# Spectral tower kernel on one core: the 32x32 tile sets wait for both pairs of PSUM banks together and go out as sixteen matmuls in one run

## The chip, the cores and the metric

The kernel runs on one core of a Trainium2 chip. The metric is the device time of one execution in microseconds (us). Three runs of the kernel before are given, beside one profiled execution. Engines: TensorE (PE, its weight loads PEld), VectorE (DVE), ScalarE (ACT), GpSimd (POOL), and SyncE (SP), which issues most transfers.

## What is computed

The reference puts 64 images of 64x64 through a small Fourier network (four layers, 32 channels), and the result through a short attention and mixture-of-experts stage on 65 tokens of 64 numbers. The part that matters here is the layer:

```python
for i in range(L):                       # L = 4
    x1 = _fourier_layer(v, W1, W2)       # rfft2, 24x12 modes mixed over channels, irfft2
    x2 = einsum('bcxy,cd->bdxy', v, w_w[i]) + w_b[i]
    v = x1 + x2
    v = batchnorm(v) * bn_g[i] + bn_b[i] # statistics over all images and positions
    if i < L - 1: v = relu(v)
```

After the layers come `q_w`, a class token, and a layernorm with the attention and the experts. Nothing of that tail is touched.

## The kernel before, in words

The maps don't fit on the chip, so each of the first three layers (`for l in range(PASSES)`, PASSES = 3) has two parts. `mix(l)` works on the modes. The pass that follows goes over the images in 16 groups of four ("quads", q = 0 to 15). It finishes layer l for the quad and begins layer l + 1: it builds the output map, clips it, stores it, transforms it forward to modes, and takes the channel product of the next layer only to gather its sum of squares, which that layer's normalisation needs.

A quad has two halves (h = 0 and 1). For each half the pass makes two sets of values in PSUM, both in banks 0 to 3:

- **Output set** (`out_set`): the channel product of layer l into banks 0 to 3, then 32 inverse-transform matmuls added to it (L1660). The channel product has three forms. In layer 0 it is four 32-row matmuls, one to a bank (L1646). In layers 1 and 2 it is `blocks32` (L1621) for q of 2 and more, and four full matmuls (L1637) for q = 0 and 1, which were kept on the chip.
- **Next set** (`next_set`): the channel product of layer l + 1 of the finished map, `blocks32` in every layer.

`blocks32` covers the 128x128 array with small matmuls of 32 rows and 32 columns; one of them (row group r, column group x) reads partitions 32r to 32r + 31 and writes bank r. Each is an fp32 matmul of 512 columns and stands in the trace as two records and two weight loads. In the kernel before it is called for a **pair** of banks: pair 0 is banks 0 and 1 (r = 0, 1), pair 1 is banks 2 and 3 (r = 2, 3), so eight matmuls per call, 16 records.

The pairs have semaphores of their own. `a_full[pair]` is raised when a pair is written, `a_free[pair]` when it has been read. `free_pair` (L1608) is the wait of TensorE for `a_free[pair]` of the set before. The readers of a set are:

| set | pair 0 | pair 1 |
|---|---|---|
| output, h = 0 | ACT relu (L1430) | DVE relu (L2036, then the clip L2039) |
| next, h = 0 | ACT square (L1439) | DVE bn_stats (L2045) |
| output, h = 1 | ACT relu (L1430) | ACT relu (L1430) |
| next, h = 1 | ACT square (L1439) | ACT square (L1439) |

So in the sets of h = 1 one engine reads pair 0 and then pair 1.

Banks 4 to 7 hold the forward transform: `y_transform` (L1683, 16 tiles of 32x32 at once, in two halves), and `x_transform` (L1695). Between them VectorE transposes (`turn_spectra`, L2074); it also transposes the finished map (`turn_map`, L2061) for `y_transform`.

TensorE runs its instructions in the order of the code. In this text the eight steps of one round are called A to H:

```python
for q in range(QUADS + 1):
    if q < QUADS: out_set(l, q, 0)          # A
    if q:
        y_transform(l, q - 1, 0)            # B
        next_set(l, q - 1, 0)               # C
        y_transform(l, q - 1, 1)            # D
    if q < QUADS: out_set(l, q, 1)          # E
    if q:
        x_transform(l, q - 1, 0)            # F
        next_set(l, q - 1, 1)               # G
        x_transform(l, q - 1, 1)            # H
```

ACT's order in a round is: relu of A (pair 0), square of C (pair 0), relu of E (both pairs), copy of F's result (L1447), square of G (both pairs), copy of H's result. DVE's order: relu and clip of A (pair 1), bn_stats of C (pair 1), two `turn_spectra`, two `turn_map`. SP stores each finished half map (L1160), loads the maps of later quads in layers 1 and 2 (L1166, awaited by `ld`), and loads the inverse spectra (L1171, awaited by `g_in`).

## Time and profile before

| | |
|---|---|
| three runs | 1352.03, 1356.14, 1361.01 us; median 1356.14 |
| the profiled execution | 1348.81 us, span of its instructions 1347.0 us |
| PE busy | 1134.5 us (84%), 18183 matmul records |
| PE weight loads | 646.0 us (48%) |
| DVE busy | 855.6 us (64%) |
| ACT busy | 551.6 us (41%) |
| POOL busy | 367.7 us (27%) |
| mean granted TensorE clock | 0.936 of full speed |

Busy time is the union of an engine's records. The idle time in square brackets of a row is that of the engine just before it, with what ended it. "issue" means that the profile shows nothing the engine waited for. Matmuls overlap in the array, so a group of x32 is one run of records.

### The profile page before, as it was taken

To read this page: it belongs to the slowest core of one execution; us is meant where nothing else is said; L and a number is where in the kernel's file an instruction comes from. 1 tells how busy PE (TensorE), PEld (TensorE's weight loads), DVE (VectorE), ACT (ScalarE), POOL (GpSimd) and SP (SyncE) were. 2 spreads that over 40 slices of the span, in tenths; PEclk is the share of its full clock that TensorE was granted. 3 is DMA by queue.
4 is the path that set the end of the run, shared out by engine and by line. 5 is a ranking of instruction groups with operands and counts; after the bars stand their busy time and mean duration, and the time that the engine had idled before them with its cause. 6 is when DMAs were issued, how large, how long until landed. Compare 5 with 4: busy or idle time off the path is not lost.

```text
span 1347.0 us, 40550 instructions
## 1 busy us (share of the span) xinstructions
PE 1134.5 (84%) x18183; PEld 646.0 (48%) x18183; DVE 855.6 (64%) x1041; ACT 551.6 (41%) x808; POOL 367.7 (27%) x533
## 2 busy tenths in 40 slices
PE   4698899999969889899996989999899677954596
PEld 4444555555534445555554445555455352223552
DVE  6576676777747566666764856666666480058664
ACT  2165454444536444444443644444444380100150
POOL 8673113224235303121422630122222351100000
PEclk9899899999989999999997999999999898976789
DMA  6568999898328999999962789999997267931001
GB/s 165 139 192 221 274 248 226 211 232 200 101 89 202 233 318 351 337 361 330 363 203 59 198 219 342 351 336 370 327 355 230 43 269 257 379 110 42 1 0 32
DMA packets 156119, 300.29 MB, mean 223 GB/s; under 512 B 33064, under 2 KB 100024, under 8 KB 139012
## 3 DMA queue, kind: packets, MB, share of 16 engines
q1 hardware_dynamic: 131656, 251.53, 60.8%
q0 software_dynamic: 20864, 44.73, 11.5%
q8 instruction: 143, 2.34, 0.7%
q10 hardware_dynamic: 3426, 1.44, 0.4%
q14 instruction: 30, 0.25, 0.1%
HBM read 147.86 MB, written 128.48 MB: 205 GB/s over the span
## 4 chain that ended last, share of the span: by engine, by line
PE 56%; DMA 12%; DVE 11%; SPq 8%; ACT 6%; issue 5%; POOL 2%; DVEq 0%; ACTq 0%; POOLq 0%
PE ps L1621 14%; PE ps L1660 10%; PE ps L1695 7%; PE ps L1683 6%; PE ps L1584 4%; SPq L1160 3%; PE ps L1646 3%; PE ps L1548 3%; DMA half_inverse<-arena 2%; DMA arena<-maps 2%; SPq L1054 1%; PE ps L1563 1%; DMA maps<-arena 1%; PE ps L1523 1%; ACT arena L1430 1%
## 5 line engine op out<-in xcount | busy, mean ns | idle before, releaser
L1660 PEld LDWEIGHTS ps<-arena 48*128 48x128 f32 x3072 | 182.2, 190 | 86.3 <-issue 82.2
L1660 PE MATMUL ps<-arena 48*128 48x128 f32 x3072 | 201.4, 281 | 7.3 <-issue 3.2
L1430 ACT ACTIVATE arena<-ps,arena 128x1024 f32<-128x1024 f32 x96 | 112.3, 1202 | 221.5 <-PE ps L1660 203.4
L1109 POOL DMA_DIRECT2D arena<-arena x207 | 120.4, 589 | 301.9 <-ACT arena L1447 298.0
L1439 ACT ACTIVATE ps<-ps 128x1024 f32<-128x1024 f32 x144 | 145.5, 1011 | 98.7 <-PE ps L1621 98.4
L2074 DVE STREAM_TRANSPOSE arena<-ps 128x1024 f32<-128x1024 f32 x96 | 177.3, 1929 | 5.5 <-PE ps L1683 5.5
L1621 PE MATMUL ps<-arena 32*32 32x512 f32 x2944 | 160.3, 616 | 9.3 <-DMA arena<-maps 5.6
L1683 PE MATMUL ps<-arena 32*32 32x512 f32 x3072 | 152.2, 599 | 5.6 <-DVE arena L2061 3.4
L2061 DVE STREAM_TRANSPOSE arena<-arena 128x2048 f32<-128x2048 f32 x64 | 144.3, 2289 | 12.8 <-issue 6.4
L1695 PE MATMUL ps<-arena 128*64 128x96 f32 x2304 | 122.8, 257 | 32.7 <-DVE arena L2074 29.8
L1695 PEld LDWEIGHTS ps<-arena 128*64 128x64 f32 x2304 | 103.7, 142 | 87.6 <-issue 47.2
L1255 POOL TENSOR_SCALAR arena<-arena 32x384 f32<-32x384 f32 x96 | 112.4, 1171 | 83.4 <-DMA arena<-in_mode_w 77.1
L2036 DVE TENSOR_SCALAR arena<-ps,arena 128x1024 f32<-128x1024 f32 x32 | 43.0, 1343 | 117.5 <-PE ps L1660 117.5
L1621 PE MATMUL ps<-inputs,arena 32*32 32x512 f32 x1920 | 107.9, 613 | 7.7 <-issue 6.7
L1548 PE MATMUL ps<-arena 64*64 64x64 f32 x2304 | 79.9, 287 | 33.2 <-DMA arena<-arena 31.0
L1430 ACT ACTIVATE inputs<-ps,arena 128x1024 f32<-128x1024 f32 x48 | 56.1, 1202 | 120.7 <-PE ps L1660 120.7
L1548 PEld LDWEIGHTS ps<-arena 64*64 64x64 f32 x2304 | 65.3, 155 | 82.8 <-issue 71.6
L1249 POOL DMA_DIRECT2D arena<-in_mode_w x48 | 26.8, 566 | 260.0 <-ACT arena L1447 242.8
L2045 DVE BATCH_NORM_STATS2 arena<-ps 128x6 f32<-128x512 f32 x96 | 62.3, 690 | 40.9 <-PE ps L1621 40.9
L2061 DVE STREAM_TRANSPOSE arena<-inputs 128x2048 f32<-128x2048 f32 x32 | 72.5, 2308 | 8.1 <-ACT inputs L1430 4.0
L1621 PEld LDWEIGHTS ps<-arena 32*32 32x32 f32 x2944 | 39.7, 104 | 79.1 <-ACT arena L1430 30.0
L1035 ACT COPY arena<-ps 128x1024 f32<-128x1024 f32 x66 | 56.2, 857 | 50.2 <-PE ps L1584 50.2
(314 smaller groups left out, 1394.4 us busy)
## 6 DMA issues: line engine op xcount, KB each, us to landing
arena<-half_inverse SPq DMA_DIRECT2D x90, 384.0 KB, 12.1
half_inverse<-arena SPq DMA_DIRECT2D x120, 256.0 KB, 4.6
maps<-arena SPq DMA_DIRECT2D x112, 256.0 KB, 4.6
maps<-inputs SPq DMA_DIRECT2D x112, 256.0 KB, 12.4
arena<-maps SPq DMA_DIRECT2D x28, 1024.0 KB, 17.3
maps<-arena SPq DMA_DIRECT2D x28, 1024.0 KB, 18.0
inputs<-maps SPq DMA_DIRECT2D x28, 1024.0 KB, 21.7
arena<-in_mode_w POOLq DMA_DIRECT2D x48, 384.0 KB, 7.2
```

The costliest lines, as they stand in the source:

```text
L1109: eng.dma_start(dst, src).then_inc((modes_st[batch % 2], last_st, late_st)[part], 16)
L1255: nc.gpsimd.tensor_scalar(w, w, -1.0, None, ALU.mult).then_inc(signed, 1)
L1430: nc.scalar.activation(half(h_out(l, q), h)[:, 1024 * pair:1024 * pair + 1024], ps[:, 2 * pair:2 * pair + 2, :].rearrange("p b n -> p (b n ...
L1439: nc.scalar.activation(src, src, ACT.Square, accum_out=sums_x2[:, i:i + 1])\
L1548: last = nc.tensor.matmul(ps[64 * e:64 * e + 64, 2 * s + m, 0:384] .rearrange("p (b k) -> p k b", b=BATCH)[:, k], ring[2 * p + e][rows, 6 ...
L1621: last = nc.tensor.matmul(ps[32 * x:32 * x + 32, r, :], w[rows, 32 * r:32 * r + 32], source[rows, at:at + 512], start=True, stop=last_one)
L1660: last = nc.tensor.matmul(ps[:, b, at:at + 128], gtile[s][rows, 4 * b + 2 * h + n, :], iy[rows, :], start=False, stop=(i >= 2 and n == 1))
L1683: last = nc.tensor.matmul(ps[32 * x:32 * x + 32, 4 + r, :], fyt[rows, yh, :], src, start=(yh == 0), stop=(yh == 1))
L1695: last = nc.tensor.matmul(ps[64 * t:64 * t + 64, 4 + b, 96 * (y - 3 * b):96 * (y - 3 * b) + 96], spectra[:, at:at + 64], fx2[:, r, :], sta ...
L2045: last = nc.vector.bn_stats(stats[:, 12 * q + 6 * b:12 * q + 6 * b + 6], ps[:, 2 + b, :])
L2061: nc.vector.transpose(dst, src).then_inc(h_turned, 1)
L2074: nc.vector.transpose(dst, src).then_inc(y_turned, 1)
```

## The change

`blocks32` no longer takes a pair. It goes over the four column groups and, within each, over all four row groups: sixteen matmuls in a run. Before it TensorE waits for both pairs. `a_full[0]` is raised by the matmul of x = 3, r = 1, and `a_full[1]` by that of x = 3, r = 3. In layer 0 the four matmuls of the output set also follow both waits. The branch of layers 1 and 2 for the two kept quads (L1637) is left as it was.

```diff
-            def blocks32(w, source, h, pair, last_one):
+            def blocks32(w, source, h, done):
+
                 for x in range(4):
-                    for r in (2 * pair, 2 * pair + 1):
+                    for r in range(4):
                         rows = slice(32 * r, 32 * r + 32)
                         at = 2048 * h + 512 * x
-                        last = nc.tensor.matmul(ps[32 * x:32 * x + 32, r, :], w[rows, 32 * r:32 * r + 32],
-                                                source[rows, at:at + 512], start=True, stop=last_one)
-                return last
+                        ins = nc.tensor.matmul(ps[32 * x:32 * x + 32, r, :], w[rows, 32 * r:32 * r + 32],
+                                               source[rows, at:at + 512], start=True, stop=done)
+                        if done and x == 3 and r % 2:
+                            ins.then_inc(a_full[r // 2], 1)
...
                     for pair in range(2):
                         free_pair(l, "out", q, h, pair)
-                        blocks32(wbd[l], h_in(l, q), h, pair, False)
+                    blocks32(wbd[l], h_in(l, q), h, False)
...
                     for pair in range(2):
                         free_pair(l, "out", q, h, pair)
-                        for g in (2 * pair, 2 * pair + 1):
-                            rows = slice(32 * g, 32 * g + 32)
-                            nc.tensor.matmul(ps[:, g, :], expconv[rows, at:at + 128],
-                                             feats[u][rows, 512 * h:512 * h + 512], start=True, stop=False)
+                    for g in range(4):
+                        rows = slice(32 * g, 32 * g + 32)
+                        nc.tensor.matmul(ps[:, g, :], expconv[rows, at:at + 128],
+                                         feats[u][rows, 512 * h:512 * h + 512], start=True, stop=False)
...
                 for pair in range(2):
                     free_pair(l, "next", q, h, pair)
-                    blocks32(wbd[l + 1], h_out(l, q), h, pair, True).then_inc(a_full[pair], 1)
+                blocks32(wbd[l + 1], h_out(l, q), h, True)
```

Lines behind L1616 move: what is L1621, L1660, L1683 and L1695 before is L1622, L1662, L1685 and L1697 after.

What TensorE's row of instructions is at steps F, G, H and the next A, in layer 1, before the change:

```order
L1695 MATMUL ps<-arena 64x96 [waits y_turned]
L1695 MATMUL ps<-arena 64x96 x11
L1621 MATMUL ps<-inputs,arena 32x512 [waits a_free0]
L1621 MATMUL ps<-inputs,arena 32x512 x7
L1621 MATMUL ps<-inputs,arena 32x512 [waits a_free1]
L1621 MATMUL ps<-inputs,arena 32x512 x7
L1695 MATMUL ps<-arena 64x96 [waits y_turned]
L1695 MATMUL ps<-arena 64x96 x11
L1621 MATMUL ps<-arena 32x512 [waits a_free0,ld_a0]
L1621 MATMUL ps<-arena 32x512 x7
L1621 MATMUL ps<-arena 32x512 [waits a_free1]
L1621 MATMUL ps<-arena 32x512 x7
```

The same place after it:

```order
L1697 MATMUL ps<-arena 64x96 [waits y_turned]
L1697 MATMUL ps<-arena 64x96 x11
L1622 MATMUL ps<-inputs,arena 32x512 [waits a_free1,a_free0]
L1622 MATMUL ps<-inputs,arena 32x512 x15
L1697 MATMUL ps<-arena 64x96 [waits y_turned]
L1697 MATMUL ps<-arena 64x96 x11
L1622 MATMUL ps<-arena 32x512 [waits a_free1,a_free0,ld_a0]
L1622 MATMUL ps<-arena 32x512 x15
```

The eight matmuls of pair 0 now stand behind the wait for pair 1, and the first matmul of the run carries one wait more.

TensorE at steps B, C and D, in layer 1, before the change:

```order
L1683 MATMUL ps<-arena 32x512 [waits y_turned,xs_ev,h_turned]
L1683 MATMUL ps<-arena 32x512 x15
L1621 MATMUL ps<-inputs,arena 32x512 [waits a_free0]
L1621 MATMUL ps<-inputs,arena 32x512 x7
L1621 MATMUL ps<-inputs,arena 32x512 [waits a_free1]
L1621 MATMUL ps<-inputs,arena 32x512 x7
L1683 MATMUL ps<-arena 32x512 [waits y_turned,xs_ev,h_turned]
L1683 MATMUL ps<-arena 32x512 x15
```

After it:

```order
L1685 MATMUL ps<-arena 32x512 [waits y_turned,xs_ev,h_turned]
L1685 MATMUL ps<-arena 32x512 x15
L1622 MATMUL ps<-inputs,arena 32x512 [waits a_free1,a_free0]
L1622 MATMUL ps<-inputs,arena 32x512 x15
L1685 MATMUL ps<-arena 32x512 [waits y_turned,xs_ev,h_turned]
L1685 MATMUL ps<-arena 32x512 x15
```

The order of the steps is unchanged; nothing moves past B or D, and ACT, DVE, POOL and SP have the same instructions in the same order.

## Rows read from the trace of the kernel before

**Rows 1.** Busy time by stretch, steady part of passes 0 and 1; columns named in row.

```profile
core 0: us, PE busy (x) PEld busy (x) DVE busy (x) ACT busy (x) POOL busy (x), PEclk, DMA share, GB/s
144.00:372.00 228.00, 219.23 (x3800) 130.96 (x3800) 167.90 (x120) 108.18 (x163) 54.82 (x82) 1.00 0.82 209
480.00:715.00 235.00, 215.66 (x4296) 122.17 (x4280) 160.38 (x113) 104.92 (x157) 54.74 (x82) 0.99 0.95 317
```

**Rows 2.** Timeline, pass 0: start us, us, engine line op, operands, count [idle before <-releaser].

```profile
190.00 1.34 DVE L2036 TENSOR_SCALAR arena<-ps,arena 128x1024 f32<-128x1024 f32 x1 [3.51 <-PE ps L1660]
190.82 0.29 PEld L1621 LDWEIGHTS ps<-arena 32*32 32x32 f32 x16 [0.78 <-ACT arena L1430]
191.40 0.18 PEld L1621 LDWEIGHTS ps<-arena 32*32 32x32 f32 x16 [0.28 <-DVE arena L2036]
191.99 1.62 PE L1683 MATMUL ps<-arena 32*32 32x512 f32 x30
192.59 1.30 DVE L2045 BATCH_NORM_STATS2 arena<-ps 128x6 f32<-128x512 f32 x2 [0.52 <-PE ps L1621]
...
196.74 2.30 ACT L1430 ACTIVATE arena<-ps,arena 128x1024 f32<-128x1024 f32 x2 [3.57 <-DMA maps<-arena]
...
198.68 0.18 PEld L1621 LDWEIGHTS ps<-arena 32*32 32x32 f32 x16
199.09 0.18 PEld L1621 LDWEIGHTS ps<-arena 32*32 32x32 f32 x16 [0.23 <-ACT arena L1430]
199.88 1.01 ACT L1439 ACTIVATE ps<-ps 128x1024 f32<-128x1024 f32 x1 [0.55 <-PE ps L1621]
...
200.89 1.02 ACT L1439 ACTIVATE ps<-ps 128x1024 f32<-128x1024 f32 x1
202.07 0.30 PEld L1646 LDWEIGHTS ps<-inputs,arena 32*128 32x128 f32 x4 [0.51 <-ACT ps L1439]
```

**Rows 3.** Timeline, pass 0, step G one round earlier, pair 1.

```profile
183.79 0.18 PEld L1621 LDWEIGHTS ps<-arena 32*32 32x32 f32 x16 [0.23 <-ACT arena L1430]
```

**Rows 4.** Timeline, passes 1 and 2, step G in five rounds.

```profile
479.67 0.18 PEld L1621 LDWEIGHTS ps<-inputs,arena 32*32 32x32 f32 x16 [0.70 <-ACT inputs L1430]
...
529.72 0.18 PEld L1621 LDWEIGHTS ps<-inputs,arena 32*32 32x32 f32 x16 [0.79 <-ACT inputs L1430]
529.95 1.01 ACT L1439 ACTIVATE ps<-ps 128x1024 f32<-128x1024 f32 x1
...
1021.35 0.18 PEld L1621 LDWEIGHTS ps<-arena 32*32 32x32 f32 x16 [0.79 <-ACT arena L1430]
...
1053.46 0.51 PEld L1621 LDWEIGHTS ps<-arena 32*32 32x32 f32 x32
```

**Rows 5.** Timeline, pass 1, ACT frees pair 0 and step E begins.

```profile
706.21 0.19 ACT L1439 ACTIVATION_READ_ACCUMULATOR ps<-ps 128x1 f32 x1
...
706.52 0.24 PEld L1621 LDWEIGHTS ps<-arena 32*32 32x32 f32 x16 [0.59 <-issue]
```

**Rows 6.** Timeline, pass 1, a step G with both pairs free.

```profile
596.88 0.23 PEld L1621 LDWEIGHTS ps<-inputs,arena 32*32 32x32 f32 x32
...
598.08 1.01 ACT L1439 ACTIVATE ps<-ps 128x1024 f32<-128x1024 f32 x1 [0.69 <-PE ps L1621]
```

**Rows 7.** Waits of the weight loads by line, passes 0, 1, 2: total us, times, longest.

```profile
PEld ps L1621 <- issue: 1.9, 2, 1.6
...
PEld ps L1621 <- issue: 15.9, 20, 2.9
...
PEld ps L1621 <- issue: 19.3, 28, 2.1
```

**Rows 8.** Timeline, end of pass 1: steps B and C, both pairs free.

```profile
715.65 0.27 PEld L1683 LDWEIGHTS ps<-arena 32*32 32x32 f32 x32 [1.32 <-DVE arena L2061]
...
716.54 0.57 PEld L1621 LDWEIGHTS ps<-inputs,arena 32*32 32x32 f32 x31 [0.33 <-issue]
...
717.92 1.01 ACT L1439 ACTIVATE ps<-ps 128x1024 f32<-128x1024 f32 x1 [2.34 <-PE ps L1621]
```

## The prediction

> **What bounds the kernel now.** I read the busy time by stretch first. In the steady part of pass 0 PE is busy 219.23 of 228.00 us and DVE 167.90; in pass 1 it is 215.66 of 235.00 and 160.38 [rows 1]. That looks like PE as the bound, but overlapping matmuls are counted as busy while they drain, so I read the timeline of one round for who waits for whom [rows 2]. The reader should follow this loop:
>
> - C: ACT frees pair 0, and PE starts it at 190.82. DVE's relu runs from 190.00 to 191.34, and PE starts pair 1 at 191.40.
> - DVE's bn_stats follow, 192.59 to 193.89, and free pair 1 for E.
> - E's relu runs on ACT from 196.74 to 199.04 (two of 1.2 us), pair 0 first. The row names a store of the maps as releaser. I set that aside: in the code the relu of A in the same round has already waited for the same value of that semaphore, so at E only E's matmuls are left to wait for.
> - G: PE starts pair 0 at 198.68, straight behind F, and pair 1 at 199.09, released by that relu.
> - ACT's squares of G start at 199.88 and 200.89, back to back, and PE starts pair 1 of the next A at 202.07, released by the second square.
>
> A round is 15.30 us long (pair 1 of G at 183.79 and at 199.09) [rows 2, 3]. In each of C, E and A, pair 1 is the late one and lies on the loop; an early pair 0 gains nothing there. G is the exception. Its pair 0 starts 0.41 us before pair 1, ACT reads both pairs in turn, and what ends last is pair 0's start plus two squares. So the early pair 0 of G is worth its whole lead.
>
> **The change part by part.** Matmuls, weight loads and bytes are the same. What changes is when pair 0 starts, how long a run is, and how many waits the first matmul has.
>
> *G waits for both pairs.* The square begins 1.20 us after the start of pair 0 (198.68 to 199.88) [rows 2]. A run of both pairs that were free together shows the same 1.20 us (596.88 to 598.08) [rows 6]. With both waits ahead the run begins at 199.09, the first square at 200.29 instead of 199.88, and everything behind it is 0.41 us later: second square, A, relu, C, bn_stats, E. Nothing hides it, since the two squares already stand back to back and A already waits for the second.
>
> In passes 1 and 2 the lead of pair 0 varies. It is the idle time in the row of pair 1 plus the 0.18 us of pair 0's own loads. I count the 30 full rounds in three classes [rows 4]. In 11 rounds the lead is 0.85 to 0.97 us, on average 0.94 (first: 0.70 + 0.18 = 0.88 at 479.67; last: 0.79 + 0.18 = 0.97 at 1021.35). These are rounds whose E came late, so that ACT was still in its relus when F was done. There the loss is also the whole lead: the square at 529.95 would start at 529.72 + 1.20 = 530.92. In 9 rounds the lead is about 0.33 (the run of 0.51 us at 1053.46, less 0.18). In the other ten it is small: eight of about 0.11, one of 0.62, and one whose cause is an instruction stall that remains, counted as nothing. Sum: 11 x 0.94 + 9 x 0.33 + 8 x 0.11 + 0.62 = 14.8 us.
>
> *A run of sixteen instead of eight from the late release.* The sixteen weight loads of a pair take 0.18 us, the 32 of both pairs 0.23 [rows 2, 6], so the last matmul starts 0.05 us later. Bounds: nothing, if the reader waits for pair 0 only, and 0.05. I take 0.05, for C and G in pass 0 and for all four sets in passes 1 and 2. The four-matmul form of layer 0 adds next to nothing.
>
> The Trainium skill's page "TensorE: Matmul & The Clock Gate", section on the measured speedup against the span model, puts each further packed tile at about 4 ns. By it eight more tiles cost 0.03 us instead of 0.05, about 3 us less in the uncovered sum; the row's 6 ns decides.
>
> *One wait more on the first matmul.* A set whose single wait ends releases PE 0.06 us later (191.34 to 191.40) [rows 2]. Where the first matmul has two waits, as at E in pass 1, the square ends at 706.40 and the loads begin at 706.52, so 0.12 [rows 5]. In the new order every set begins with two waits or more, the late one among them. I charge the difference, 0.06 us, four times a round. Bounds: 0, if the late wait is still taken last and directly, and 0.12.
>
> *Sum.* A round of pass 0 gets 0.41 + 2 x 0.05 + 4 x 0.06 = 0.75 us longer. Thirteen of its 15 rounds are of that kind, and two had another hold-up at G and pay 0.34: 10.4 us. Passes 1 and 2 pay 14.8 + 30 x 4 x 0.11 = 28.0 us if nothing covers it.
>
> *What may cover it.* In pass 1 the DMA queues are at a share of 0.95 (0.82 in pass 0) [rows 1], and the loads of L1621 wait 15.9 us in 20 places, and 19.3 us in 28 in pass 2, for nothing the profile names, against 1.9 us in 2 in pass 0 [rows 7]. I take these for instructions that arrive late behind the data. A PE that comes later at such a place waits less there, so a delay ahead of it is partly paid already. No row says how large a part; with 20 and 28 such waits in some 14 rounds each, there are one or two a round to pay into, but not behind every delay. I let half of the 28.0 go: 14.0 us. Bounds: none and all of it.
>
> Together 10.4 + 14.0 = 24.4 us on the profiled execution's 1348.8 (span 1347.0 and 1.8 around it), so 1373. The median of the runs, 1356.1, stands 7.3 above that execution; the same step gives 1380, which is 1.8% slower. A measurement of this kernel can tell about 1%, 13.6 us, from no change.
>
> **The rivals.**
>
> *Nothing is covered, or the stalls grow.* PE used to pass pair 0 early and so called for its next instructions early; now it stands in front of the set and then takes sixteen matmuls in a burst. For it: stalls of up to 2.9 us inside such sets [rows 7]. Against it: PE also has longer to be supplied. Price: 38.4 us, 1394.
>
> *The busy passes cover all.* If late data and late instructions pace passes 1 and 2, their rounds stay as long as they are, and only pass 0 pays: 10.4 us, 1366, under 1%. For it: DMA share 0.95. Against it: many rounds there have the same closed loop of G, squares and A, with no wait for DMA in it.
>
> *Not slower: PE's array time decides.* Where both pairs are free when PE arrives, two half runs are worse than one, because pair 1 queues behind pair 0 while a y_transform is still in the array. At the end of pass 1 B starts at 715.65 and the square of C at 717.92, 2.27 us [rows 8]; at most 1.0 us for the B run and the 1.20 above would give 2.20 or less, so 0.1 to 0.3 us saved at C and the like at E behind D. That decides from the point where PE, not ACT or DVE, is last at C and E. With 0.3 us in each of 30 rounds and the loss at G gone (both pairs free there too) it is -9 us, 1347. Against it: in the round of rows 2 PE waits 0.78 us for pair 0 of C and 0.28 for pair 1, and D is done at 193.61, before bn_stats at 193.89. The skill's same section speaks for this rival: sixteen packed tiles of 32x32 cost hardly more than one. The trace agrees (1.20 us for eight and for sixteen), but the array isn't what the loop waits for.
>
> That the change doesn't do what it says is excluded by the new order of the instructions.
>
> **How the numbers follow.** Forecast, half covered (a quarter to three quarters: 1373 to 1388): 0.50. Nothing covered, 1394: 0.17. All covered, 1366: 0.20. Not slower, 1347: 0.08. The remaining 0.05 is for what I don't see, on both sides. Slower by over 1% takes the first two and a part of the rest, 0.68; within 1% the next two, 0.28; faster by over 1% 0.04. The range of 1362 to 1395 leaves out the last rival, and the tail of the worst. The likeliest is 1380.
>
> **What would show it.** In the profile after, G has one run of 32 loads behind ACT's second relu, and the first square starts about 1.25 us behind that; the round of pass 0 is 16.05 instead of 15.30 (15.8 would mean that the additional wait costs nothing); PE waits about 0.4 to 0.5 us more a round for ACT's square (A), and DVE as much more for A's L1662. The waits of L1622 on nothing named should shrink in passes 1 and 2; if they don't, the first rival is right. I am wrong if the round of pass 0 stays at 15.30, if the squares of G aren't back to back any longer, or if the granted clock of the steady stretches falls from 1.00 and 0.99 (2.4 GHz), since PE now stands idle longer before each A.

## The result, and the profile after

The changed kernel takes 1403.34 us (median of 4 runs, 1400.87 to 1411.13) where the kernel before takes 1357.01 (4 runs, 1352.03 to 1361.01): a ratio of 1.0347, 95% interval 1.030 to 1.0393. It is 3.5% slower. The forecast had 1380 and a range of 1362 to 1395: the sign was right, the time lies outside the range, and the forecast had half of the loss that came. The ratios here and below leave out the few executions that took over 1.5% longer than the fastest of the same kernel.

The profiled execution of the changed kernel takes 1401.0 us (span 1399.2, mean granted clock 0.927), so it stands 52.2 above that of the kernel before. In what follows "a round" is one q, and the steps are A to H as ahead of the prediction. A pass is measured from the last matmul of its first set to the release of its last one. Read so, the three passes take 273.4, 287.7 and 294.6 us, against 256.2, 274.0 and 272.8: 17.2, 13.7 and 21.8 us more. That is the whole difference; between the passes and behind them nothing moved by more than half a microsecond. (How far the single passes can be trusted is a question for before_again below.)

The busy time by stretch, kernel after, answers [rows 1]:

```profile
core 0: us, PE busy (x) PEld busy (x) DVE busy (x) ACT busy (x) POOL busy (x), PEclk, DMA share, GB/s
144.00:372.00 228.00, 184.16 (x3552) 109.11 (x3550) 157.46 (x112) 101.71 (x152) 45.87 (x66) 0.99 0.84 206
480.00:715.00 235.00, 188.59 (x3938) 107.41 (x3938) 149.81 (x105) 96.61 (x144) 46.87 (x67) 0.98 1.01 322
```

PE falls from 219 to 184 busy microseconds in pass 0, although a round has the same matmuls. Most of that isn't lost time: before, pair 0's run filled the stretch in which pair 1 was waited for, and now PE stands idle there and the same matmuls stand closer together. What is lost shows on DVE, 168 to 157 in pass 0 and 160 to 150 in pass 1, which does the same work per round: rounds are 6 to 7% longer. The granted clock of each stretch is 0.01 lower than before.

Two groups of section 5 of the pages (line, operation, operands, count, busy and mean, idle ahead and its releaser). The kernel before:

```profile
L1439 ACT ACTIVATE ps<-ps 128x1024 f32<-128x1024 f32 x144 | 145.5, 1011 | 98.7 <-PE ps L1621 98.4
L2045 DVE BATCH_NORM_STATS2 arena<-ps 128x6 f32<-128x512 f32 x96 | 62.3, 690 | 40.9 <-PE ps L1621 40.9
```

and the kernel after:

```profile
L1439 ACT ACTIVATE ps<-ps 128x1024 f32<-128x1024 f32 x144 | 145.5, 1011 | 158.9 <-PE ps L1622 158.9
L2047 DVE BATCH_NORM_STATS2 arena<-ps 128x6 f32<-128x512 f32 x96 | 62.3, 690 | 46.6 <-PE ps L1622 46.6
```

The readers of the next layer's products wait longer for them: ACT 158.9 us in all instead of 98.7, DVE 46.6 instead of 40.9.

The timeline of one round of pass 0, kernel after, with the columns of [rows 2], from one C over the next G to the bn_stats of the next C:

```profile
196.00 0.27 PEld L1622 LDWEIGHTS ps<-arena 32*32 32x32 f32 x32 [1.42 <-ACT arena L1430]
...
201.63 2.30 ACT L1430 ACTIVATE arena<-ps,arena 128x1024 f32<-128x1024 f32 x2 [3.20 <-PE ps L1662]
...
204.04 0.27 PEld L1622 LDWEIGHTS ps<-arena 32*32 32x32 f32 x32 [0.71 <-issue]
204.07 1.15 PE L1622 MATMUL ps<-arena 32*32 32x512 f32 x32 [0.55 <-ACT arena L1430]
205.36 1.01 ACT L1439 ACTIVATE ps<-ps 128x1024 f32<-128x1024 f32 x1 [1.14 <-PE ps L1622]
206.37 1.02 ACT L1439 ACTIVATE ps<-ps 128x1024 f32<-128x1024 f32 x1
207.61 0.34 PEld L1648 LDWEIGHTS ps<-inputs,arena 32*128 32x128 f32 x8 [1.44 <-issue]
207.64 1.14 PE L1648 MATMUL ps<-inputs,arena 32*128 32x512 f32 x8 [1.28 <-ACT ps L1439]
210.89 1.34 DVE L2038 TENSOR_SCALAR arena<-ps,arena 128x1024 f32<-128x1024 f32 x1 [4.33 <-PE ps L1662]
212.35 0.27 PEld L1622 LDWEIGHTS ps<-arena 32*32 32x32 f32 x32 [1.42 <-ACT arena L1430]
212.38 1.15 PE L1622 MATMUL ps<-arena 32*32 32x512 f32 x32 [0.54 <-DVE arena L2038]
213.66 1.01 ACT L1439 ACTIVATE ps<-ps 128x1024 f32<-128x1024 f32 x1 [2.00 <-PE ps L1622]
213.72 1.30 DVE L2047 BATCH_NORM_STATS2 arena<-ps 128x6 f32<-128x512 f32 x2 [0.76 <-PE ps L1622]
```

C begins at 196.00 and again at 212.35: the undisturbed round is 16.35 us, where the prediction said 16.05 and the kernel before has 15.30 [rows 2, 3]. Going along it against [rows 2]:

- **C.** DVE's relu ends at 210.89 + 1.34 = 212.23, and the first load starts at 212.35, 0.12 behind it (0.06 before). The matmul starts another 0.03 behind its load. The bn_stats start 1.37 behind the load (192.59 - 191.40 = 1.19 before). Together 0.24 us more from relu to bn_stats.
- **G.** The relu of both pairs ends at 201.63 + 2.30 = 203.93; load at 204.04, square at 205.36. From relu to square that is 1.43, against 199.88 - 199.04 = 0.84: 0.59 more, of which 0.41 is the lead that pair 0 had.
- **A.** The second square ends at 207.39 and the load starts at 207.61, 0.22, against 202.07 - 201.91 = 0.16; with the 0.03 to the matmul some 0.1 more.
- **E.** By the same working from the trace 0.11 more.

0.24 + 0.59 + 0.10 + 0.11 = 1.04 of the 1.05 us. The form "one run of 32 loads behind ACT's second relu, then squares back to back" is as forecast; the joint set is dearer than forecast at every place.

The waits of the weight loads, kernel after, answer [rows 7]: those of L1622 on nothing named, in the steady parts of passes 0, 1 and 2 (us in total, times, longest), then those of L1648 (A and E) in pass 0:

```profile
PEld ps L1622 <- issue: 11.8, 16, 1.3
...
PEld ps L1622 <- issue: 47.2, 44, 1.5
...
PEld ps L1622 <- issue: 48.1, 44, 3.4
...
PEld ps L1648 <- issue: 39.6, 29, 1.4
```

The prediction said that these waits would shrink. In passes 1 and 2 they grew to 2.5 to 3 times what they were [rows 7], but the row doesn't mean what I had taken it for. At 204.04 the load waited 0.71 us "for issue" while the matmul behind it waited for ACT: it is the wait for the relu, under another name. Run late_first below shows why.

### The profile page after: what moved, and what is told of

The parts are those of the page before. It is cut to its first block, busy times and chain, and to the rows that moved or that the text cites. A ratio compares the mean times of both kernels' runs of the same rounds, so it can differ in the third digit from the quotient of the medians.

```text
span 1399.2 us, 40678 instructions
## 1 busy us (share of the span) xinstructions
PE 1081.0 (77%) x18183; PEld 620.0 (44%) x18183; DVE 855.0 (61%) x1041; ACT 552.1 (39%) x808; POOL 367.2 (26%) x533
## 3 DMA queue, kind: packets, MB, share of 16 engines
q8 instruction: 144, 2.36, 0.7%
## 4 chain that ended last, share of the span: by engine, by line
PE 49%; DVE 16%; ACT 16%; issue 8%; DMA 6%; SPq 3%; POOL 1%; DVEq 0%; ACTq 0%; POOLq 0%
PE ps L1622 13%; PE ps L1662 12%; ACT ps L1439 7%; ACT arena L1430 4%; PE ps L1584 4%; PE ps L1548 3%; DVE arena L2038 3%; DMA maps<-arena 3%; PE ps L1648 2%; ACT inputs L1430 2%; PE ps L1639 2%; DVE arena L2047 2%; PE ps L1697 2%; PE ps L1563 2%; SPq L1086 2%
## 5 line engine op out<-in xcount | busy, mean ns | idle before, releaser
L1662 PEld LDWEIGHTS ps<-arena 48*128 48x128 f32 x3072 | 187.2, 193 | 95.1 <-issue 93.6
L1662 PE MATMUL ps<-arena 48*128 48x128 f32 x3072 | 207.9, 285 | 12.7 <-issue 10.4
L1439 ACT ACTIVATE ps<-ps 128x1024 f32<-128x1024 f32 x144 | 145.5, 1011 | 158.9 <-PE ps L1622 158.9
L1622 PE MATMUL ps<-arena 32*32 32x512 f32 x2944 | 116.8, 620 | 51.0 <-ACT ps L1439 16.5
L1697 PE MATMUL ps<-arena 128*64 128x96 f32 x2304 | 126.4, 262 | 31.0 <-DVE arena L2076 26.5
L1697 PEld LDWEIGHTS ps<-arena 128*64 128x64 f32 x2304 | 106.5, 145 | 86.4 <-issue 49.9
L1685 PE MATMUL ps<-arena 32*32 32x512 f32 x3072 | 135.0, 608 | 8.6 <-issue 8.5
L2038 DVE TENSOR_SCALAR arena<-ps,arena 128x1024 f32<-128x1024 f32 x32 | 43.0, 1343 | 139.4 <-PE ps L1662 139.4
L1622 PE MATMUL ps<-inputs,arena 32*32 32x512 f32 x1920 | 76.9, 609 | 41.0 <-ACT ps L1439 17.8
L1249 POOL DMA_DIRECT2D arena<-in_mode_w x48 | 26.8, 564 | 284.5 <-ACT arena L1447 267.5
L2047 DVE BATCH_NORM_STATS2 arena<-ps 128x6 f32<-128x512 f32 x96 | 62.3, 690 | 46.6 <-PE ps L1622 46.6
L1622 PEld LDWEIGHTS ps<-arena 32*32 32x32 f32 x2944 | 28.4, 104 | 103.0 <-issue 64.7
```

The lines of the kernel that those rows point to most:

```text
L1439: nc.scalar.activation(src, src, ACT.Square, accum_out=sums_x2[:, i:i + 1])\
L1622: ins = nc.tensor.matmul(ps[32 * x:32 * x + 32, r, :], w[rows, 32 * r:32 * r + 32], source[rows, at:at + 512], start=True, stop=done)
L1662: last = nc.tensor.matmul(ps[:, b, at:at + 128], gtile[s][rows, 4 * b + 2 * h + n, :], iy[rows, :], start=False, stop=(i >= 2 and n == 1))
L1685: last = nc.tensor.matmul(ps[32 * x:32 * x + 32, 4 + r, :], fyt[rows, yh, :], src, start=(yh == 0), stop=(yh == 1))
L1697: last = nc.tensor.matmul(ps[64 * t:64 * t + 64, 4 + b, 96 * (y - 3 * b):96 * (y - 3 * b) + 96], spectra[:, at:at + 64], fx2[:, r, :], sta ...
L2047: last = nc.vector.bn_stats(stats[:, 12 * q + 6 * b:12 * q + 6 * b + 6], ps[:, 2 + b, :])
```

## The experiments

Each group of kernels ran on one chip with the kernel before beside them, so each ratio is to the kernel before of the same group. There are ten runs. The diffs show the heart of each edit; `...` stands for like edits elsewhere and for helper functions that only spell out a loop over a pair or over both.

In every run whose steady round was forecast, the round came within 0.15 us of it. The times didn't fit as well: they were off by up to 19 us, on either side. What is said of the round of pass 0 is therefore better founded than what is said of the whole time.

### The part of step G: g_split and g_only

g_split is the changed kernel with G's pairs apart again; g_only is the kernel before with G alone joined.

```diff
 def next_set(l, q, h):
+    if h == 1:
+        for pair in range(2):
+            free_pair(l, "next", q, h, pair)
+            pair32(wbd[l + 1], h_out(l, q), h, pair)
+        return
...
```

> The kernel after, with the next set of h = 1 (step G) alone back in two pairs with their own waits. Theory: of the 1.05 us by which a round of pass 0 grew (15.30 to 16.35), 0.59 lie at G: the lead of pair 0 of 0.41 and 0.18 of costs of a joint set. So the round should be 15.76 us, and the kernel about 28 us shorter than after, some 1373 to 1375. Rival: a run of sixteen matmuls is itself slow, the same in each of the four sets of a round, and the lead of pair 0 counts for little; then taking one of four away gives back a quarter, a round of 16.09 and about 1390 us.

Measured: 1389.56 us (1377.36 to 1408.34, 5 runs), ratio 1.0236 (1.0134 to 1.0338). The steady round of pass 0 is 15.65, so G gives back 0.70 of the 1.05 us, and the three passes take 262.5, 284.0 and 288.9. The round speaks for the theory (15.76 against 16.09); the median is that of the rival (1390), and 15 us above the theory's. Passes 1 and 2 gave back 3.7 and 5.7 us in the profiles, less than G's leads there; how much of that is chance can't be told from one profile (see before_again).

```diff
 def next_set(l, q, h):
+    if h == 1:
+        for pair in range(2):
+            free_pair(l, "next", q, h, pair)
+        joint32(wbd[l + 1], h_out(l, q), h)
+        return
...
```

> The kernel before, with step G alone made joint: both waits, then sixteen matmuls. Theory: a round of pass 0 of 15.30 + 0.59 = 15.89 us, and about 28 us more than before in the whole, some 1385. Rival (every joint set costs alike): 15.56 us and about 1369.

Measured: 1374.66 us (4 runs), ratio 1.0145 (1.0073 to 1.0216), round 15.90. G joined in the kernel before costs 0.60 us a round, as the theory had it; the time is 10 us under the theory's. The timeline of g_only, one G of pass 0:

```profile
198.42 2.30 ACT L1430 ACTIVATE arena<-ps,arena 128x1024 f32<-128x1024 f32 x2 [3.56 <-DMA maps<-arena]
...
200.83 0.28 PEld L1630 LDWEIGHTS ps<-arena 32*32 32x32 f32 x32 [0.61 <-issue]
202.15 1.01 ACT L1439 ACTIVATE ps<-ps 128x1024 f32<-128x1024 f32 x1 [1.14 <-PE ps L1630]
```

Relu to square is 202.15 - 200.72 = 1.43, as in the kernel after, and C, E and A are as in the kernel before. So the effects are separable: the losses of g_only and g_split are 1.45% and 2.36%, together 3.8% against 3.5% for the whole. What follows: the lost lead at G is real, but with its 0.41 us it is less than half of the 1.05. The rest is a dearer joint set, at G itself and at the three sets where, by the prediction, pair 0's early start was worth nothing.

### The order of the two waits: late_first

A set that waits for both pairs names pair 0 and then pair 1 in the code, and pair 1 is the late one. Here the late one is named first, in output sets and next sets alike. In the output sets both waits also move ahead of those for the inputs (`conv_exp` and `f_in` in layer 0, `ld` in layers 1 and 2), which stood first.

```diff
 def next_set(l, q, h):
-    for pair in range(2):
+    for pair in (1, 0):
         free_pair(l, "next", q, h, pair)
     blocks32(wbd[l + 1], h_out(l, q), h, True)
...
```

> The kernel after, with nothing changed but the order of the waits in the code before each joint set: pair 1 (the late one) first, pair 0 and the loads behind it, so that the wait that ends last is carried by the first weight load and not by an instruction of its own ahead of it. Theory: that instruction costs 0.07 us a set, so a round of pass 0 of 16.35 - 4 x 0.07 = 16.07 and about 12 us less in the whole, 1391. Rival: two waits cost the same in either order, 16.35 and 1403.

Measured: 1382.22 us (1377.97 to 1384.87, 4 runs), ratio 1.019 (1.0122 to 1.0258), against 1.0347: about 1.5% of the time back for the order of the waits. The round is 16.00 (16.07 was expected), the time 9 us under the theory's. The timeline of late_first, one C of pass 0:

```profile
192.23 1.34 DVE L2038 TENSOR_SCALAR arena<-ps,arena 128x1024 f32<-128x1024 f32 x1 [4.06 <-PE ps L1662]
...
193.63 0.24 PEld L1622 LDWEIGHTS ps<-arena 32*32 32x32 f32 x32 [1.36 <-DVE arena L2038]
193.63 1.15 PE L1622 MATMUL ps<-arena 32*32 32x512 f32 x32 [0.45 <-DVE arena L2038]
...
194.98 1.30 DVE L2047 BATCH_NORM_STATS2 arena<-ps 128x6 f32<-128x512 f32 x2 [0.68 <-PE ps L1622]
```

The relu ends at 193.57 and the load starts 0.06 behind, as in [rows 2]; its matmul starts with it, not 0.03 later. That is 0.09 us a set, and four sets make the 0.35 us of the round. Where the late wait had been shows in the instructions at L1610, the line of that wait, over the same 244 us of pass 0. Kernel after:

```profile
L1610 PEldq EVENT_SEMAPHORE  x88: 51/51/51, 146.3 to 385.9; - x88
```

and late_first:

```profile
L1610 PEldq EVENT_SEMAPHORE  x30: 51/51/51, 152.4 to 385.1; - x30
```

Which semaphore each record waits for is in the trace as well, though the views above leave it out. In the kernel after, the weight load of C and G carries the wait for pair 0, and a separate instruction ahead of it, 51 ns long, waits for pair 1. At A and E the load carries the wait for `conv_exp`, the first in the code, pair 0 has a separate instruction, and pair 1 shares one with the input. So the first wait of the code is carried by the weight load itself, and the others sit on instructions of their own ahead of it. Of the 88 rows, 30 at C and G and 29 at A and E name pair 1: but for one, these are four sets in 15 rounds, and every joint set has its late wait in the slow place. In late_first none has. Its 30 rows at L1610 name pair 0, which is free earlier, at C and G, and the separate instructions of A and E stand at the lines of the waits for the inputs. The kernel before has 29 rows here, all at A and E, and none names pair 1.

This also explains the rows above. In late_first the waits of L1648 have their names back:

```profile
PEld ps L1648 <- ACT ps L1439: 19.4, 14, 1.4
PEld ps L1648 <- DVE arena L2047: 18.6, 15, 1.2
```

19.4 + 18.6 = 38.0 us in 29 waits, where the kernel after shows 39.6 "for issue" in 29. A wait that ends on the separate instruction isn't the load's own, and the profile finds no releaser for it, or a wrong one: at C the row of 212.35 names ACT, which freed pair 0 about 0.6 us before, where DVE's relu is what ended the wait. In late_first the same wait stands under DVE L2038, 20.2 us in 15 places.

### The same wait without joint sets: two_waits

The kernel before, with one more wait ahead of pair 1's, for pair 0, which is long satisfied. It puts the late wait of each pair 1 in the second place; the matmuls stay as they are.

```diff
 def free_pair(l, kind, q, h, pair):
     if SETS[kind, q, h]:
+        if pair:
+            pe.wait_ge(a_free[0], set_of(l, kind, q, h))
         pe.wait_ge(a_free[pair], set_of(l, kind, q, h))
```

> The kernel before, with a second wait, one that is long satisfied (that of pair 0), ahead of the wait of pair 1, in every set; the first weight load of pair 1 carries the satisfied one. Matmuls stay in pairs. Theory: pair 1 is late on the loop in C, E and A, each by 0.07 us, and not at G: a round of pass 0 of 15.30 + 0.21 = 15.51 and 9 us more than before, 1366. Rival: a wait more costs nothing, 15.30 and 1357; then the costs of a joint set are all in its sixteen matmuls.

Measured: 1384.72 us (1378.87 to 1399.15, 4 runs), ratio 1.0227 (1.0137 to 1.0317), round 15.47. The timeline of two_waits, a C of pass 0:

```profile
193.32 1.34 DVE L2038 TENSOR_SCALAR arena<-ps,arena 128x1024 f32<-128x1024 f32 x1 [4.41 <-PE ps L1662]
...
194.78 0.21 PEld L1623 LDWEIGHTS ps<-arena 32*32 32x32 f32 x16 [0.34 <-issue]
...
196.00 1.30 DVE L2047 BATCH_NORM_STATS2 arena<-ps 128x6 f32<-128x512 f32 x2 [0.60 <-PE ps L1623]
```

Relu to load is again 0.12 and load to bn_stats 1.22 instead of 1.19, with pairs apart. So the 0.09 belongs to the wait's place and not to the run of sixteen. Of four such sets a round only 0.17 us reaches the round, not 0.35. The working for that is at split_late. But the time rose by 2.3%, far more than 45 rounds of 0.17, and 19 us more than expected: the passes take 264.0, 286.5 and 299.4 in the profiled execution, which was the slowest of the four. In pass 2 the loads wait longer for nothing named. Two_waits:

```profile
PEld ps L1623 <- issue: 34.2, 56, 3.7
PEld ps L1662 <- issue: 27.2, 30, 1.7
```

Much of the first row is the misnamed wait again, in 56 places. I also added up the intervals of over 0.6 us from the start of one TensorE record to the start of the next, where the next has no wait at all; these can't be misnamed. Below they are called stalls, though a part of each is the array at work. In the three passes they come to 6.3, 16.5 and 32.9 us, against 2.6, 12.0 and 16.9 in the kernel before. Why the third pass of this kernel has twice the stalls isn't explained.

### Which part of the time is pass 0: pass0_only

The change applied in pass 0 alone.

```diff
 def next_set(l, q, h):
+    if l:
+        for pair in range(2):
+            free_pair(l, "next", q, h, pair)
+            pair32(wbd[l + 1], h_out(l, q), h, pair, True)
+        return
...
```

> The change in pass 0 alone; passes 1 and 2 in pairs as before. The changed kernel's profile has pass 0 longer by 17.2 us, pass 1 by 13.7 and pass 2 by 21.8. Theory: each pass pays by itself, in every round, and nothing covers it: pass 0 at 273.4 us against 256.2, passes 1 and 2 at about 273 each as before, in the whole 17 us more than before, some 1369 to 1371. Rival: part of what passes 1 and 2 lost comes down to them from pass 0 (the clock, the stores of pass 0 still under way), then they grow here too and the time is nearer 1385.

Measured: 1375.91 us (1370.4 to 1382.64, 4 runs), ratio 1.014 (1.0041 to 1.024). Pass 0 is 273.5 us and its round 16.35, as in the kernel after. The clean loop of pass 0, which the forecast put at 10.4 us, costs 17.3. The passes that keep the old order take 284.0 and 279.0 in this execution, 10 and 6 us more than in the first profile of the same instructions, so the profile alone doesn't exclude the rival. The median is 5 us above the theory's and 9 under the rival's, and the interval has room for both. That asked for a control.

### How far the busy passes vary by themselves: before_again

> The kernel before, unchanged, as a control. The steady round of pass 0 should be 15.30 us again and pass 0 256 us within 1. What is open is how far the stalls of PE inside its runs in passes 1 and 2 (12.0 and 16.9 us in the first profile) vary for the same instructions. If they are a property of the program, they come out within 3 us of these numbers, and the larger stalls of the experiments are caused by their edits. If they vary from one execution to the next, they come out off by 5 us or more in one of the passes, and differences of that size between the profiles of two kernels say nothing. The time is 1357 within its usual 0.7% either way.

Measured: 1362.42 us (1349.5 to 1368.19, 10 runs), ratio 1.0023 (0.9986 to 1.006), as it must. Its passes take 254.7, 278.4 and 276.2 us, its steady round is 15.30. Its stretch of pass 1, against [rows 1]:

```profile
core 0: us, PE busy (x) PEld busy (x) DVE busy (x) ACT busy (x) POOL busy (x), PEclk, DMA share, GB/s
480.00:715.00 235.00, 214.17 (x4207) 121.05 (x4194) 155.02 (x111) 100.78 (x152) 54.08 (x81) 0.97 0.99 315
```

The same instructions get 155.02 us of DVE work done there instead of 160.38. The stalls on PE come to 0.7, 18.0 and 18.7 us, where the first profile had 2.6, 12.0 and 16.9. The second case of the expectation holds: in one execution the stalls of a busy pass are worth no more than plus or minus 6 us. With pass0_only there are three profiles of the old order in passes 1 and 2: 274.0, 278.4 and 284.0 us, and 272.8, 276.2 and 279.0. So a busy pass of one profile is known to 10 us, and the first profile, from which the prediction was made, has the shortest of both. Pass 0 varies by 1.5 us in all and its steady round by 0.01, so everything below 10 us in this study is read from the round of pass 0 or from medians.

With that scale, the stalls of the kernel after, 3.4, 15.6 and 18.2 us, can't be told from those of the kernel before. They didn't shrink by the 14 us that the forecast had let them take up, and they didn't grow.

### Who is late behind a joint set: r_swapped, pair_major and roles

From load to bn_stats, C has 1.19 before and 1.35 even in late_first. The sixteen-load run explains 0.05 of that. The suspicion: both pairs are now signalled within a few nanoseconds (13 by the ends of the matmuls in the trace, which are modelled), and the second signal is passed on late. The rival was that ACT and DVE, which now start on the two pairs of PSUM at the same time, are in each other's way. r_swapped takes the row groups in the order 2, 3, 0, 1, so that pair 1 is signalled first.

```diff
-                    for r in range(4):
+                    for r in (2, 3, 0, 1):
```

> The kernel after, with the row groups of the joint run in the order 2, 3, 0, 1 instead of 0, 1, 2, 3, so that the signal of pair 1 is raised 13 ns before that of pair 0 and not behind it. At step C in the changed kernel VectorE begins its bn_stats 0.19 us behind the last matmul of pair 1, where it was 0.10 before. Theory: two signals raised within 13 ns are passed on one after the other, and the second is late; then VectorE is back at 0.10 here, C's part falls by 0.09 us, and ScalarE's square of C and of G starts up to 0.09 later, so the round stays about 16.35. Rival: both readers start on PSUM at once and the second to start is held up by the first; then VectorE's delay stays what it is, or goes to whoever starts second. Time within 5 us of after in both.

The timeline of r_swapped, a C of pass 0:

```profile
195.74 0.28 PEld L1622 LDWEIGHTS ps<-arena 32*32 32x32 f32 x32 [1.42 <-ACT arena L1430]
...
197.06 1.30 DVE L2047 BATCH_NORM_STATS2 arena<-ps 128x6 f32<-128x512 f32 x2 [0.70 <-PE ps L1622]
197.12 1.01 ACT L1439 ACTIVATE ps<-ps 128x1024 f32<-128x1024 f32 x1 [2.07 <-PE ps L1622]
```

In the kernel after ACT starts 1.31 behind the load and DVE 1.37; here DVE starts 1.32 behind it and ACT 1.38. Over the rounds of pass 0 (medians at C), ACT starts 145 ns behind the end of its pair and DVE 192 in the kernel after; swapped, it is 190 and 146. (In the kernel before 37 and 104.) The delay goes with the order of the signals. At C that doesn't decide, since the reader that is signalled second also starts second, and the expectation gave this outcome to the rival as well. G decides: ACT alone reads both pairs there. Its first square starts 107 ns behind the end of pair 0 in the kernel before and 146 in the kernel after, where pair 0 is signalled first; swapped, where it is signalled last, it is 191, with no other reader of these banks to be in its way. So the rival falls. DVE's return to 104, which the theory had, didn't come. The time didn't change: 1403.77 us (2 runs), ratio 1.036 (1.0231 to 1.0488), round 16.35.

pair_major keeps both waits ahead but issues pair 0's eight and then pair 1's eight, so the signals are 62 ns apart.

```diff
-                for x in range(4):
-                    for r in range(4):
+                for x, r in [(x, 2 * pair + i) for pair in range(2) for x in range(4) for i in range(2)]:
```

> The kernel after, with both waits ahead of the run as there, but the eight matmuls of pair 0 first and then the eight of pair 1. The two signals then are some 50 ns apart instead of 13, and pair 0 is full 40 ns earlier. Theory (what a joint run costs is its start and its length): pair 0 of G is full 0.04 us earlier and VectorE's delay at C shrinks from 0.19 to about 0.12, a round of pass 0 of about 16.25. Rival (the order over row groups matters for how fast the array takes sixteen): the round moves by more than 0.15 either way.

A miss. ACT's delay falls to 93 ns, but DVE's stays at 192, where about 0.12 us was expected; 1403.81 us (2 runs), ratio 1.036 (1.0224 to 1.0496). The round of the profile is 16.40, but it can't be held against the 16.25 expected: this execution had a lower granted clock throughout, never over 0.95 where all the other profiles reach 1.00. Its steady part of pass 0:

```profile
144.00:388.00 244.00, 200.76 (x3792) 117.59 (x3792) 167.70 (x120) 108.02 (x161) 54.88 (x82) 0.94 0.80 196
```

The packed matmuls take 618 ns there instead of 588, and A and E, which the edit doesn't touch in pass 0, are 0.04 us longer each. Without these the round would be 16.32 or less (an estimate from these rows); whether the edit gains at full clock is open.

What is shown: behind a joint set DVE, signalled last, starts some 90 ns later than in the kernel before (192 against 104), ACT as the one signalled last just as late (190, against 37 at C and 107 at G), and 62 ns between the signals don't help. Why is open; being closer than 62 ns isn't the condition.

roles is the kernel before with the readers exchanged where h is 0: DVE takes pair 0 and ACT pair 1, so that the longer pair of operations starts first. It was the one idea in the study for a kernel better than both.

```diff
-                for pair in range(2 if h else 1):
+                for pair in (0, 1) if h else (1,):
...
```

> The kernel before, matmuls in pairs, with the readers of the sets of h = 0 exchanged: VectorE (relu 1.34 us, clip, bn_stats 1.30) takes pair 0, which an output set fills 0.45 us before pair 1, and ScalarE (relu 1.20, square 1.01 + 0.19) takes pair 1. No arithmetic is left out. Theory (the loop goes through whichever pair of C is free last): VectorE frees pair 0 at about the time at which ScalarE freed it before, plus 0.15, ScalarE frees pair 1 about 0.15 earlier than VectorE did, bn_stats start up to 0.45 earlier, and E waits for ScalarE's square, ready about 0.25 us earlier than bn_stats were. A round of pass 0 of 15.05 us and 10 us less than before, 1344. Rival: the loop is closed by another limb (turn_spectra, F, G), and the round stays at 15.30.

The round of pass 0 falls to 15.04, as expected, and pass 0 to 251.1 us. The time is 1352.74 us (median of 10 runs, one of which was far off at 2432.93), ratio 0.9968 (0.9921 to 1.0016): no difference that can be told, where 10 us were expected. In this profile pass 1 took 284.5 us, and its stalls came to 25.4.

### Both costs taken back: split_late

g_split and late_first in one kernel: G in pairs, and the three joint sets C, E and A with the late wait first (and, as in late_first, ahead of those for the inputs).

> The kernel after with both costs taken back that the earlier runs separated: G waits pair by pair again (g_split), and the three joint sets C, E and A take their late wait first in the code (late_first). If the two costs are independent, the steady round of pass 0 is g_split's 15.65 less three times the 0.09 us that late_first gained per joint set, 15.38, and the time is g_split's 1389.6 less three quarters of late_first's gain of 21.1 us, 1374. Rival: the gain of late_first comes from G alone (from the lead that G loses); then the round stays at 15.65 and the time within 5 us of 1389.

Measured: 1369.47 us (1360.18 to 1385.67, 12 runs), ratio 1.0076 (1.0041 to 1.0111); passes 261.3, 275.0 and 284.4. The rival falls, by the time and by the round (15.65 in g_split): the order of the waits gains with G in pairs as well. The time is within 5 us of what was expected. The round is 15.48 and not 15.38, and the trace tells why. The timeline of split_late, a G of pass 0:

```profile
199.46 2.30 ACT L1430 ACTIVATE arena<-ps,arena 128x1024 f32<-128x1024 f32 x2 [3.11 <-DMA maps<-arena]
...
201.39 0.18 PEld L1632 LDWEIGHTS ps<-arena 32*32 32x32 f32 x16
...
201.81 0.18 PEld L1632 LDWEIGHTS ps<-arena 32*32 32x32 f32 x16 [0.24 <-ACT arena L1430]
202.59 1.01 ACT L1439 ACTIVATE ps<-ps 128x1024 f32<-128x1024 f32 x1 [0.54 <-PE ps L1632]
```

The first loads of G (201.39) follow F without idle time; their wait, for the first of the two relus, ended long before. What times them is F ahead of them on PE, not the relu, so the square at 202.59 hangs on F. A relu of E that comes 0.11 later is caught there: from that relu to the release of G is 2.87 us in g_split and in two_waits, 2.96 in split_late, 2.98 in the kernel before. In a kernel with G in pairs, a delay at E is free, up to the lead. So removing it gains nothing. What three sets gain, 3 x 0.09, less the 0.09 that G loses, is the 0.17 us by which the round is shorter than g_split's 15.65; in two_waits the same sum appears with the other sign. With G joined there is no such cover, and all four sets pay. That part of G's price was in no step of the prediction.

What is left of split_late over the kernel before, 15.48 - 15.30 = 0.18 us, stands at C (0.05 for the run of sixteen, about 0.1 for the later second reader). Forty-five rounds of it are 8 us, and by the ratio the time is 10 above.

## Why the prediction was right or wrong

**The loop and the place.** Right. The chain of G, its two squares, A, C's relu, bn_stats and E sets the round before and after. Pair 0's lead at G is worth its whole length: g_only gives 0.60 a round for G, of which 0.41 is left when the terms below (0.09, 0.05, 0.04) are taken off. Early pairs 0 in E and A gain nothing by themselves: in late_first, where the late wait is carried directly, E and A are each only 0.01 us longer than in the kernel before.

**A run of sixteen, 0.05.** Right in size. The loads of both pairs take 0.24 us in late_first, where the wait is carried directly, and those of one pair 0.18 before. At C and at G it reaches the reader.

**One wait more, 0.06 four times a round.** Too small. It is 0.09: 0.06 until the load, as read from [rows 5], and 0.03 more until the matmul, which no row of the prediction held. late_first measures it directly, 0.35 us in four sets. The bounds given for this step were 0 and 0.12, and they hold; 0 was for the case that "the late wait is still taken last and directly". It is taken last and not directly.

**The second reader.** Missing from the sum. About 0.09 us at C, and 0.04 at G: two signals at the end of one run, where there had been one behind each. The Trainium skill's page "TensorE: Matmul & The Clock Gate", section on the per-tile semaphore tail, says that increments at the end of a packed group serialize, at about 26 ns each. One increment more in the group of C would by that figure cost 1.2 us in 45 rounds, an estimate from the page. The trace doesn't agree in size: the reader signalled last is 88 ns later than before, and stays so with the signals 62 ns apart.

Together the joint sets cost 0.64 us a round beside the lead, where the sum had 0.34.

**Half of it covered in passes 1 and 2.** This is the step that failed worst. It read, "I let half of the 28.0 go: 14.0 us", because the loads of L1621 wait there for instructions [rows 7]. With the sizes measured in pass 0 the two passes should lose 14.8 for the leads and 30 x 0.64 = 19.2, so 34.0 us uncovered (an estimate; the sizes weren't read in these passes). The first two profiles show 13.7 + 21.8 = 35.5, but that agreement is partly luck, since a busy pass of one profile is known to 10 us. The medians are the better witness: 46.3 us for the whole, less 17.3 for pass 0, leave 29.0 for passes 1 and 2, and with the interval of the ratio 23 to 36. So they lost twice the 14.0, and of the 34.0 nothing to a third was covered, not half. The stalls inside PE's runs show no difference beyond their own 6 us either. The mistake is in the reasoning, too: a stall that appears in a place where PE has nothing else to wait for doesn't get shorter because PE arrives later, unless its instructions were on their way meanwhile, and no row said that they were. (That is argument: no run shows what the stalls wait for.) I had written "No row says how large a part" and then took the middle; the rows for a part of nothing were as good.

**The sum.** On the profiled executions the forecast had +24.4 and the change brought +52.2. Of the 27.8 between them, 14.0 is the cover, 6.8 is pass 0 (17.2 instead of 10.4; 15 x 0.30 = 4.5 from the larger joint sets, the rest from the two rounds that I had counted as held up by something else and from outside the steady rounds), 6.0 is the same 0.64 for 0.44 in the other two, and 1.0 is left. The medians stand 46 apart, since the profiled execution of the kernel before was 8.2 under the median of its four and that of the kernel after 2.3 under its own. By the medians 22 us were missing from the forecast: 7 in pass 0, 6 for the larger joint sets of passes 1 and 2, and 9 for the cover.

**The rivals.** The first, that nothing is covered, had 1394 and 0.17, and was the nearest in both mechanism and time, but its reason, stalls that grow, isn't borne out. Its sign, waits on nothing named that don't shrink, came, but for another reason, the place of the wait. Its price was too low as well, since it took the same sizes per set. The second, all covered, is excluded. The third needs a PE that comes late to free pairs: in pass 1 of the kernel after, L1622 waited in 44 places for nothing named, by the reading of late_first mostly for a release. How often its case came up wasn't counted; the time excludes it as the main effect. The granted clock, which I had named as a danger, stayed at 0.99 and 0.98 in the steady stretches (2.4 GHz nearly throughout) although PE stands idle longer before each A. At the very start of pass 0 it is another matter. That stretch of the kernel after:

```profile
129.80:147.00 17.20, 14.03 (x133) 8.98 (x146) 8.70 (x6) 4.61 (x4) 5.57 (x8) 0.50 0.91 250
```

PE has the lower of its two levels (1.2 GHz) for all of it; in the kernel before the mean there is 0.80. No run separates what this costs; the first rounds of pass 0 are not visibly longer for it, and the whole of pass 0 leaves 1.4 us beside 15 x 1.05.

**What stays open.** What sets the length of the stalls in passes 1 and 2, and their 33 us in pass 2 of two_waits; how much of the loss these passes covered, between nothing and a third; and what delays the second reader.

## What to carry to other kernels

A joint wait costs the lead of the earlier resource only where the reader takes both in turn, but it also removes the slack that this lead gave to the steps ahead of it. Where a TensorE instruction must wait for two things, name the one that comes last first in the code, and look afterwards whether its wait still carries the name of its releaser in the profile; a "wait for issue" that is as long as the wait it replaced is that wait. Don't count an idle time as cover for a delay unless a row shows what goes on during it. And look at the granted clock and at a second profile of the same kernel before reading a few microseconds out of one.

## What the runs showed of the hardware

The place of a wait is worth 0.09 us. The first wait in the code is carried by the weight load, the others by instructions ahead of it (semaphores in the traces of the kernel after and late_first). A weight load that carries the wait starts 0.06 us after the releasing instruction's end, and its matmul with it. Through the separate wait instruction the load follows after 0.12 and the matmul after 0.15 (212.23, 212.35 and 212.38 in the kernel after; 193.57, 193.63 and 193.63 in late_first). One wait more, satisfied long ago, ahead of each late wait made a kernel otherwise unchanged 2.3% slower (two_waits, 1.4 to 3.2%); 8 us of that are accounted for by the place of the late wait, the rest isn't explained.

Of two signals at the end of a joint run of matmuls, the reader of the second starts 190 to 201 ns behind the modelled end of its pair, ACT or DVE alike, and that of the first 93 to 155 ns; with signals in separate runs it was 104 ns for DVE and 37 (at C) or 107 (at G) for ACT.

Passes 1 and 2 differed by 3 to 10 us between profiled executions with the same instructions in them (before, before_again, pass0_only). One profiled execution had a granted clock of 0.95 where the others had 1.00, and its packed matmuls took 618 ns instead of 588 (pair_major).
